# Layer 1 attention in a two-layer transformer kernel: where batch 0's queries are turned, and in which steps batch 1's queries and first maxima stand

## The reference, cut to what matters

```python
x = x + _L0_xattn_ref(_layernorm(x), ctx, ctx, mask0, ...)
x = x + _L0_ffn_ref(_layernorm(x), ...)          # 8 experts, one per token
x = x + _L1_xattn_ref(_layernorm(x), ctx, ctx, mask1, ...)
x = x + _L1_ffn_ref(_layernorm(x), ...)          # one shared, 7 routed experts, two per token

# layer 1 attention
q = layer_norm(query_antecedent @ Wq, gq, bq)    # per token, before the heads are split
k = layer_norm(key_antecedent @ Wk, gk, bk)
v = layer_norm(value_antecedent @ Wv, gv, bv)
sim = einsum('bhqd,bhkd->bhqk', qh / sqrt(dk), kh)
weights = softmax(sim + bias)                    # 16 heads of 16 channels
```

## Time and profile before

| | |
|---|---|
| median of three runs | 548.04 us |
| profiled execution | 548.11 us |
| its span, first to last instruction | 546.9 us |
| PE busy | 504.9 us, 92% |
| DVE busy | 261.6 us, 48% |
| ACT busy | 207.3 us, 38% |
| layer 0's FFN, last PE instruction | 219.58 us from the start |
| layer 1 attention, from its first top to the shared expert | 225.4 to 324.9 us |

### The profile page before, as it was taken

How to read it: one execution, slowest core, us unless ns; L and a number is a source line. 1 busy time by engine, 2 the same in 40 slices (tenths; PEclk the granted TensorE clock), 3 DMA queues, 4 the chain that set the end, 5 groups by cost and what they waited for, 6 DMA issues and landing times.

```text
span 546.9 us, 8791 instructions
## 1 busy us (share of the span) xinstructions
PE 504.9 (92%) x3285; PEld 373.3 (68%) x3285; DVE 261.6 (48%) x789; ACT 207.3 (38%) x425; POOL 82.2 (15%) x108
## 2 busy tenths in 40 slices
PE   2999999999889999679699998999999999999995
PEld 1456555645778999546356435656799999999994
DVE  5567798673337364365577826161322222222220
ACT  2434645462346653225466662220122222222221
POOL 2400700002102110200000000017212122212222
PEclk9999999997999999859899999999999999999999
DMA  8500005997113230380000012009786677666712
GB/s 299 188 1 0 2 1 164 369 373 224 59 38 104 72 97 20 99 296 1 0 2 2 1 39 77 1 10 362 269 282 201 202 238 248 211 200 220 251 13 33
DMA packets 42435, 72.06 MB, mean 132 GB/s; under 512 B 3405, under 2 KB 33037, under 8 KB 42384
## 3 DMA queue, kind: packets, MB, share of 16 engines
q1 hardware_dynamic: 33648, 60.65, 32.5%
q0 software_dynamic: 4336, 6.75, 5.6%
q10 hardware_dynamic: 4400, 4.01, 2.3%
HBM read 56.88 MB, written 14.51 MB: 131 GB/s over the span
## 4 chain that ended last, share of the span: by engine, by line
PE 57%; DVE 5%; DMA 3%; issue 2%; ACT 1%; POOL 1%; POOLq 0%; ACTq 0%; DVEq 0%
PE PS L1817 16%; PE PS L1832 9%; PE PS L1726 6%; PE PS L764 4%; PE PS L774 4%; PE PS L1737 3%; PE PS L1614 3%; PE PS L1603 3%; PE PS L795 2%; DVE W L956 2%; DMA VR<-scratch_rows 1%; PE PS L364 1%; PE PS L349 1%; PE PS L333 1%; PE PS L808 1%
## 5 line engine op out<-in xcount | busy, mean ns | idle before, releaser
L956 DVE TENSOR_REDUCE W<-PS 128x2 f32<-128x512 f32 x128 | 84.7, 687 | 41.3 <-PE PS L764 40.6
L1817 PE MATMUL PS<-PR,W 128*128 128x128 f32 x836 | 96.5, 275 | 0.0
L1817 PEld LDWEIGHTS PS<-PR,W 128*128 128x128 f32 x836 | 94.9, 192 | 0.1
L764 PE MATMUL PS<-W 32*128 32x256 f32 x512 | 85.7, 432 | 3.1 <-issue 1.6
L774 PE MATMUL PS<-W 32*128 32x512 f32 x256 | 84.3, 672 | 0.7 <-ACT W L1084 0.7
L764 PEld LDWEIGHTS PS<-W 32*128 32x128 f32 x512 | 56.4, 201 | 18.5 <-DVE W L956 9.0
L1832 PE MATMUL PS<-W,PR 128*128 x228 | 52.5, 380 | 0.8 <-ACT PR L2461 0.8
L2512 POOL DMA_INDIRECT out<-PR,slots x19 | 29.6, 1560 | 128.6 <-ACT PR L2461 125.4
L1084 ACT ACTIVATE PR<-PS 128x512 f32<-128x512 f32 x64 | 34.9, 595 | 30.8 <-PE PS L774 30.6
L1832 PEld LDWEIGHTS PS<-W,PR 128*128 128x128 f32 x228 | 41.9, 190 | 6.1 <-issue 1.2
L1084 ACT ACTIVATE W<-PS 128x512 f32<-128x512 f32 x64 | 34.7, 595 | 24.0 <-PE PS L774 24.0
(11 more groups left out here) (260 smaller groups left out, 625.5 us busy)
## 6 DMA issues: line engine op xcount, KB each, us to landing
W<-in_rguT SPq DMA_DIRECT2D x19, 1408.0 KB, 6.1
W<-in_L_ffn_W SPq DMA_DIRECT2D x16, 512.0 KB, 9.6
W<-in_rdT SPq DMA_DIRECT2D x5, 768.0 KB, 9.5
W<-in_mask SPq DMA_DIRECT2D x3, 1024.0 KB, 14.3
scratch_rows<-W SPq DMA_DIRECT2D x1, 2860.0 KB, 14.8
VR<-scratch_rows SPq DMA_DIRECT2D x19, 130.0 KB, 5.3
scratch_x<-W SPq DMA_DIRECT2D x1, 2048.0 KB, 14.1
PR<-scratch_x SPq DMA_DIRECT2D x16, 128.0 KB, 2.2
```

What stands on the lines that cost most here:

```text
L764: m = pe.matmul(PS[:, bank, q * FK:(q + 1) * FK], QT[r:r + 32, g, c:c + 128], KT[r:r + 32, g, b * FK:(b + 1) * FK], start=True, stop=True)
L956: dve.tensor_reduce(NM[:, s % 2, q:q + 2, c], PS[:, m_bank(use), :].rearrange("p (q n) -> p q n", q=2), AX, ALU.max).then_inc(sem("m_free" ...
L1817: m = pe.matmul(PS[:, bank, j * 128:(j + 1) * 128], W[:, o:o + 128], XS[:, r % 2, k, :], start=(k == 0), stop=(k == 1))
```

## The change

Four parts. **(a)** In layer 0's FFN the norms of batch 0's rows move from tile 12 to tile 11 and are shared by DVE and ACT, their turn to `beside(12)`, the projection to `mid(13)`, the second norms to `beside(13)`, and the four head groups are turned in tiles 14 and 15 instead of behind the fork. Three of four `mask_keys` go to tile 10, one to tile 14. **(b)** Batch 1's rows: the DVE pieces run on into step 0 (two per top), ACT's norms move to (0,1), the turn to (0,2), the projection to (1,0). **(c)** Batch 1's second norms and first head group move from (1,3) to (2,2), the second group stays in (2,3), third in (3,3), fourth in (4,3); the statistics of step 1 run two pieces per top from gap 1 on. **(d)** Step 4's first four tops move from gaps 2 and 3 of step 2 to step 3, whose gaps 0 and 1 then have four tops each. `pe_pairs` writes the gaps out; in gap 2 of every step of both layers a top now stands ahead of each weights job, as it did in gap 0.

```diff
-                (0, 7, 1): ["rows0_0_1"], (1, 0, 0): ["x1_1_1"]}
-    BESIDE_E = {..., (1, 0, 0): ["x1_1_0"], (1, 0, 2): ["q1_1_0", "q1_1_1"]}
-    BESIDE_E.update({(1, 1 + g, 3): [f"q1t1_{g}"] for g in range(NG)})
+                (0, 7, 1): ["rows0_0_1"], (1, 0, 2): ["x1_1_1"]}
+    BESIDE_E = {..., (1, 0, 2): ["x1_1_0"], (1, 1, 0): ["q1_1_0", "q1_1_1"],
+                (1, 2, 2): ["q1t1_0"], (1, 2, 3): ["q1t1_1"], (1, 3, 3): ["q1t1_2"], (1, 4, 3): ["q1t1_3"]}
+    def tops_of(l, n, gap):
+        if (l, n) == (1, 2) and gap > 1:
+            return []
+        if (l, n) == (1, 3) and gap < 2:
+            return [(4, i) for i in range(4 * gap, 4 * gap + 4)]
+        s, first = (n + 1, 4 + 2 * gap) if gap < 2 else (n + 2, 2 * gap - 4)
+        return [(s, i) for i in (first, first + 1) if s < STEPS]
...
+    def pe_pairs(l, n, gap):
+        tops = tops_of(l, n, gap)
+        if gap % 2:
+            pe_weights(l, n, 2 * gap)
+            pe_weights(l, n, 2 * gap + 1)
+            for s, i in tops:
+                pe_scores(l, s, i)
+            return
+        for k in range(2):
+            for s, i in tops[k:k + 1]:
+                pe_scores(l, s, i)
+            pe_weights(l, n, 2 * gap + k)
+        for s, i in tops[2:]:
+            pe_scores(l, s, i)
...
-    def dve_step(l, n, v, late):
+    def dve_step(l, n, v, late, pieces=1, since=0):
         for gap in range(4):
+            for s, i in tops_of(l, n, gap):
+                dve_top(l, s, i)
+                if gap >= since:
+                    for _ in range(pieces):
+                        next(late, None)
...
 act_beside, layer 1
-            if (n, gap) == (0, 0):
+            if (n, gap) == (0, 1):
+                act_x1(1)
+            elif (n, gap) == (0, 2):
                 act_xt_ring("x1_1", 1)
-            elif (n, gap) == (0, 2):
+            elif (n, gap) == (1, 0):
...
+            elif (n, gap) == (2, 2):
+                act.wait_ge(sem("stats"), NORMS[True]["q1_1"])
+                act.wait_ge(sem("wz"), 16)
+                for j in range(4):
+                    normal_act("q1_1", j, heads(RB[1][:, j, :]), by_head(RW[:, j, :])).then_inc(sem("q1_rows"), 1)
+                act_late_queries(0)
+            elif 2 <= n < 5 and gap == 3:
+                act_late_queries(n - 1)
...
 fast_pe, mid(i)
+            elif i == 13:
+                pe.wait_ge(sem("wp_2"), 16)
+                project_batch("q1_0", "x1_0", 2, 0)
+            elif i == 15:
+                claim(7, "q1t0_2")
+                filled(7, turned_heads(7, RB[0], 2))
+                pe.wait_ge(*at(1, "qt", 1))
+                turned_heads(5, RB[0], 3).then_inc(sem("q_ps"), 1)
 fast_pe, beside(i)
-            elif i == 13:
+            elif i == 12:
                 pe.wait_ge(sem("x1_rows"), 4)
                 turn_batch("x1_0", rows_for(0, 0))
             elif i == 14:
-                pe.wait_ge(sem("wp_2"), 16)
-                project_batch("q1_0", "x1_0", 2, 0)
+                taken(6, "q1_0")
+                taken(7, "q1_0")
+                turned_heads(5, RB[0], 0).then_inc(sem("q_ps"), 1)
+                claim(6, "q1t0_1")
+                filled(6, turned_heads(6, RB[0], 1))
...
+        pe.wait_ge(*at(1, "qt", 2))
+        taken(6, "q1t0_1")
+        taken(7, "q1t0_2")
         fork(pe, 0)
     def second_pe():
-        for g in range(NG):
-            turned_heads((5, 2, 0, 1)[g], RB[0], g).then_inc(sem("q_ps"), 1)
         pe_first(1)
...
 fast_act, beside(i)
+            elif i == 11:
+                act.wait_ge(sem("stats"), NORMS[True]["x1_0"])
+                for j in (2, 3):
+                    normal_act("x1_0", j, OB[:, 0, j, :], X[:, j, :]).then_inc(sem("x1_rows"), 1)
             elif i == 12:
-                act_x1(0)
+                act_xt("x1_0", (6,), 0)
             elif i == 13:
-                act_xt("x1_0", (6,), 0)
+                ...
+                normal_act("q1_0", 0, heads(RB[0][:, 0, :]), by_head(half(6, 0))).then_inc(sem("q1_half"), 1)
+                freed(6, normal_act("q1_0", 1, heads(RB[0][:, 1, :]), by_head(half(6, 1))))
+            elif i == 14:
+                queries_out(1, 0, 5).then_inc(sem("qt"), 1)
+                act.wait_ge(*full(6, "q1t0_1"))
+                freed(6, queries_turned(1, 0, 1, 6))
+            elif i == 15:
+                act.wait_ge(*full(7, "q1t0_2"))
+                freed(7, queries_turned(1, 0, 2, 7))
+                act.wait_ge(*at(1, "q_ps", 2))
+                queries_turned(1, 0, 3, 5).then_inc(sem("qt"), 1)
...
 second_act
-        for g in range(NG):
-            queries_out(1, g, (5, 2, 0, 1)[g]).then_inc(sem("qt"), 1)
         stored(act, TILES0)
-        act_x1(1)
 second_dve
-        dve_first(1, beside, late)
-        whole(late)
+        dve_first(1, nothing, begun)
         for s in range(8):
-            late = queries_norm() if s == 1 else rows_early() if s == 6 else empty
-            dve_step(1, s, v, late)
+            late = begun if s == 0 else queries_norm() if s == 1 else rows_early() if s == 6 else empty
+            dve_step(1, s, v, late, 2 if s < 2 else 1, 1 if s == 1 else 0)
```

More of the change, by code:

```diff
@@ L271, in ring_uses @@
             for n in range(STEPS):
-                tops = [("top", l, n + 1, i) for i in range(4, 8)] + [("top", l, n + 2, i) for i in range(4)]
                 for gap in range(4):
-                    m += [top for top in tops[2 * gap:2 * gap + 2] if top[2] < STEPS]
+                    m += [("top", l, s, i) for s, i in tops_of(l, n, gap)]
                     m += BESIDE_M.get((l, n, gap), [])
@@ L1035, in dve_beside @@
         else:
-            if (n, gap) == (0, 0):
+            if (n, gap) == (0, 2):
                 dve_xt_ring("x1_1", 1)
@@ L1039, in dve_beside @@
                 rows_taken_dve(1, 0)
-    def dve_step(l, n, v, late):
+    def dve_step(l, n, v, late, pieces=1, since=0):
         for gap in range(4):
[L1044 to L1048, removed]
+            for s, i in tops_of(l, n, gap):
[3 more added lines that the diff above has]
+                        next(late, None)
                 if gap == 1 and i == 6 and n > 1:
                     dve_divide(l, n - 2, v)
+            if gap == 1 and n > 1 and not tops_of(l, n, gap):
+                dve_divide(l, n - 2, v)
             if gap == 2 and n + 1 < STEPS:
@@ L1969, in again_pe @@
         pe.wait_ge(sem("again_rows"), 12)
+        for g in range(NG):
+            turned_heads((5, 2, 0, 1)[g], RB[0], g).then_inc(sem("again_turned"), 1)
+        pe.wait_ge(sem("again_xt"), 2 + NG)
     def second_pe():
-        for g in range(NG):
-            turned_heads((5, 2, 0, 1)[g], RB[0], g).then_inc(sem("q_ps"), 1)
         pe_first(1)
@@ L2058, in beside @@
                 settle(v, dve.tensor_scalar(masked1[:, :, :], masked1[:, :, :], 0.0, -1.0e30, ALU.is_equal, ALU.mult))
+            elif i == 10:
+                for n in range(3):
+                    dve.wait_ge(*at(1, "kt", n + 1))
+                    mask_keys(1, n)
             elif i == 11:
@@ L2062, in beside @@
                 whole(statistics(v, "x1_0", rows_of(0)))
+                for j in range(2):
+                    normal_dve("x1_0", j, OB[:, 0, j, :], X[:, j, :]).then_inc(sem("x1_rows"), 1)
             elif i == 12:
[L2064 to L2066 removed]
+                dve_xt("x1_0", 0)
             elif i == 13:
[L2068 to L2069 removed]
                 raw = [half(6 + j // 2, j) for j in range(4)]
                 whole(statistics(v, "q1_0", raw, True, [full(6 + j // 2, "q1_0") for j in range(4)]))
[L2073 to L2079 removed]
+                dve.wait_ge(sem("pads"), 3)
+                normal_dve("q1_0", 2, heads(RB[0][:, 2, :]), by_head(half(7, 2))).then_inc(*v.up())
+                freed(7, normal_dve("q1_0", 3, heads(RB[0][:, 3, :]), by_head(half(7, 3))))
+            elif i == 14:
+                dve.wait_ge(*at(1, "kt", 4))
+                mask_keys(1, 3)
+        ffn0_dve(MAIN, beside)
         fork(dve, 1, v)
@@ L2097, in second_dve @@
         empty = iter(())
-        late = queries_begun(v)
-        def beside(i):
-            if i > 2:
-                next(late, None)
         def queries_norm():
@@ L2179, in fast_act @@
         ffn0_act(MAIN, beside)
-        act.wait_ge(sem("stats"), NORMS[True]["q1_0"])
-        for j in range(2):
-            ins = normal_act("q1_0", j, heads(RB[0][:, j, :]), by_head(half(6, j)))
-            if j == 0:
-                ins.then_inc(sem("q1_half"), 1)
-        freed(6, ins)
         fork(act, 2)
@@ L2200, in again_act @@
             normal_act("q1_0", j, heads(RB[0][:, j, :]), by_head(half(6 + j // 2, j))).then_inc(sem("again_rows"), 1)
+        for g in range(NG):
+            act.wait_ge(sem("again_turned"), 3 + g)
+            queries_turned(1, 0, g, (5, 2, 0, 1)[g]).then_inc(sem("again_xt"), 1)
     def second_act():
-        for g in range(NG):
-            queries_out(1, g, (5, 2, 0, 1)[g]).then_inc(sem("qt"), 1)
         stored(act, TILES0)
```

(1 more changed line is left out.)

60 lines of the change are left out of this document (20 added, 40 removed).

## The result

The change made the kernel a little slower. Its median is 550.87 us (15 runs, 548.33 to 553.18) against 548.04 (15 runs, 546.09 to 552.12), and the ratio is 1.0042, 95% interval [1.0023, 1.0061]. The same kernel timed again beside later runs gave 1.0024 [0.9989, 1.006], which by itself can't be told from no change. The forecast was 5.4 us faster, so the prediction was wrong in its sign. The profiled execution took 550.92 us (span 549.7).

What follows compares the result with a forecast made beforehand. It took PE, waiting on chains of statistics, norms and turn, as the bound, with DVE setting the pace from 230 to 235 us. Wins of 2.6, then 4.7, then 5.4 us by step 4 gave 548.1 - 5.4 = 542.7 us, range 539.5 to 546.3.

Steps and rivals of the forecast that it cites:

- Waiting for the rows: Layer 0, after down(11): PE waits 0.3 us for the norms of batch 0's rows, ready at 202.2.
- some of the first eight ... will wait: Layer 1's first tops, no longer mixed with combines, make DVE wait: 0 to 2.5 us, taken as 1.5.
- the wait on the added maxima: Step 2's first weights wait for DVE's second statistics and added maximum: a new wait of 1.6 us, bounds 0 and 2.6.
- the wait was right: Step 2: PE waits 2.7 us for norms standing behind gap 2's exponentials, bounds 1.5 and 5.1.
- the rival of a second fall: New waits of 1.6 and 2.7 us make the clock fall around step 2: +2, 544.7 us; chance 0.17.
- the sign that the prediction named: A clock row below 0.9 after step 2's start would show the prediction wrong.
- Cost 2.3 us: Step 3's gaps 0 and 1, with eight reductions and a division, cost 2.3 us more; nearest bounds 0.8 and 4.
- The ring rule: Step 3: tops wait for banks, so the last goes out 5.3 us into the step; gaps 0 and 1 usually take 2.96.
- A clock that stays high: Rival: the clock stays high in layer 1's first phase, saving part b's 1.5 us: 541.2 us; chance 0.17.
- The long low stretch through steps 1 to 3 (558): Rival: PE stays at the low clock from the first phase through steps 1 to 3: +15, 558 us; chance 0.06.
- A slow DVE: Rival: 16 reductions in steps 1 and 3 cost 0.2 us more each, both maxima waits grow: +3.3, 546.0 us; chance 0.12.
- The reorder of gap 2: The new order in gap 2 of all 16 steps costs 0 us, bounds -1 and +1.

Runs made afterwards that it cites:

- mix_d: table_mix with part d added, the head group left in step 1's gap 3: ratio to the kernel before 0.9986 [0.9961, 1.0012].
- a_only: The changed kernel with parts b, c and d undone, the new order of gap 2 kept: ratio to the kernel before 0.9961 [0.9929, 0.9992].
- ab_table: ab with one added Exp on ACT, so the exponential's table loads before layer 1: ratio to the kernel before 0.9916 [0.9882, 0.9951].
- table_mix: ab_table with batch 1's combines begun behind step 0's sixth top, not the ninth reduction: ratio to the kernel before 0.9868 [0.9832, 0.9903], median 543.91 us.
- mix_all: table_mix with parts c and d added, so all four parts: ratio to the kernel before 0.9986 [0.9962, 1.001].
- ab_c21: ab with the second norms and first head group in step 2's gap 1, tops at old places: ratio to the kernel before 0.9951 [0.9923, 0.9978].
- mix_c21: table_mix with the second norms and first head group in step 2's gap 1: ratio to the kernel before 0.99 [0.9874, 0.9926].
- ab: The changed kernel with parts c and d undone: ratio to the kernel before 0.9946 [0.9921, 0.997].
- ab_d: The changed kernel without part c, the first head group turned in (1,3) again: ratio to the kernel before 1.0047 [1.0015, 1.0079].
- table_busy: ab_table with 40 added transposes of the identity on PE among the first tops and gaps of step 0: ratio to the kernel before 1.029 [1.025, 1.0329].
- after_rows: The changed kernel with step 3's tops ordered 0, 1, 4, 5 in gap 0 and 2, 3, 6, 7 in gap 1: ratio to the kernel before 0.999 [0.9966, 1.0014].

## Why the prediction was wrong

The forecast named moments; against those of the profiled execution the 8.2 us between 542.7 and 550.92 split as follows.

**Part a: right in mechanism and size.** Waiting for the rows cost 1.28 us instead of 0.3 (the fourth combine waited 1.14 us for a gathered row that the sum took as present), the fork 0.92 as taken. The twelve profiles that hold part a without that late row have 24.2 to 24.6 us from tile 12 to the first top against 27.1: 2.4 to 2.9 won, forecast 2.6. In this execution the first top came at 224.40, not 222.8; 1.6 us of the miss are here. 0.7 of it stood already when tile 11 began (195.13 instead of 194.47), the late row made the rest. It is late in mix_d too (1.21 us), and in no other profile. That slipping gathers cost nothing did not hold in a_only's profile, where the combines come early.

**Part b: a price left out, and one too small.** From the first top to the statistics' end the forecast has 19.4 us and the trace 22.3. The step that failed is "some of the first eight ... will wait: 0 to 2.5 us, I take 1.5". In the timeline DVE's idle times between its first reduction and the statistics' end sum to 3.9 us. The table load of 1.28 us was in no term. It had been hidden behind ACT's norms, and moving the norms uncovered it: 1.1 to 2.0 us (ab_table). Beginning the combines earlier brings the turn to the 21.7 us that the forecast had (table_mix), so the rest was DVE standing idle among tops that nothing was mixed with. By step 2's first weights the kernel is 2.5 us behind the forecast, the wait on the added maxima being 1.2 us, forecast 1.6.

**Part c: the wait was right, its tail was not.** PE waited 2.53 us, forecast 2.7. But step 2 then took 13.7 us (265.93 to 279.63) instead of 11.85. By the pieces of the timeline about 1.3 us of that is the low clock behind the wait (outputs 1.94 instead of 1.06, weights and head group slower in like measure), and about 0.6 is gap 0, whose first two weights run without the top that went ahead of them. So the rival of a second fall came in mechanism (+2 there, the whole 1.9 here with the other piece), and with it the sign that the prediction named, a clock below 0.9 after step 2's start. With it the part won nothing (mix_all against mix_d, and in its other form ab_c21 and mix_c21). That rival, with a chance of 0.17, belonged into the forecast: the clock had been at 0.50 behind the old 5.1 us wait too, and its own text said that step 2 has little work around the waits.

**Part d: the term that was mis-sized.** "Cost 2.3 us", bounds 0.8 and 4. This is the step that failed most clearly: the price is 4.4 us in this profile and 4.7 to 6.5 in the timed kernels. The ring rule was right, the last top waited 0.66 us for a bank. But the sum ended the price when that top goes out, 5.3 us into the step. It went out at 6.3 (285.95), since in gap 0 the third and fourth top already ran one behind the other and in gap 1 the first tops ran behind the weights; and its own time, 1.05 us until the outputs start at 287.00, was in no term. Those two pieces are the 2.1 us that are missing. The late top ran alone, 1.13 us for four matmuls where the three tops issued together took 1.15 for twelve. The lower bound of 0.8 us as four tops' own time was too low for the same reason. That the timed kernels say more than the profile fits a clock that falls within step 3 in part of the executions; how often it falls is not shown. No rival had that: each fall was tied to a wait of microseconds, and this one comes in a stretch with 4.95 of 5.50 us busy.

The four pieces 1.6, 2.5, 1.9 and 2.1 sum to 8.1 us. By the timed kernels, free of one profile's chances, the steps from the kernel before over ab and ab_d to the changed one are: a and b -0.54% (3.0 us), d +1.01% (5.5 us), c -0.05%. The forecast had 7.7 us won ahead of d's 2.3, so more than half of the miss, 4.5 us, lies in a to c, where 3.2 came.

**The rivals.** A clock that stays high: no, 0.50 from about 228 us to 252. The long low stretch through steps 1 to 3 (558) did not come either; the 2.9 us wait was followed by 0.60 in the mean of 248 to 253 us and 1.00 from 253 to 258; that rival's 3.5 us more for the projection was an estimate that no run shows, the projection took 3.72 us here (254.51) against 3.62 before. A slow DVE: not in this form. The wait for step 2's maxima was 1.2 us, under its forecast, and in step 3's gap 1 it is DVE that stands idle for 1.81 us until the three tops are there. (Its sum also counted 16 reductions where steps 1 and 3 have 6 and 8.) The reorder of gap 2 shows nothing: steps 4 to 7 last as before.

What stays open: why the clock falls in step 3's gap 1 in four profiles and not in the other three, and what c and d would cost with no wait of PE ahead of them at all. A version of d with a fourth bank in the M ring, which would take the wait away, was not tried, as all eight banks of the kernel's `PS` are in use.

## What to carry to other kernels

When work is moved away from in front of an instruction, list what was hidden behind it, one-time costs such as the table load of 1.28 us here among them, and give them a cheap early place. Ask of a job that is cheap beside its neighbours whether it is still issued with them: in gap 1 of step 3, with three banks for a burst of four tops, the first three took 1.15 us together and the fourth waited 0.66 us and took 1.13 alone. Bursts of three on rows that their neighbours leave free are what to try; the only burst of three run here was on shared rows in part, and it won nothing. And a term that is cheap "because it runs beside other work" deserves an upper bound at its price alone, also at the low clock: for a top 1.13 us at 1.00 and 2.07 at 0.50 here.

## What the runs showed of the hardware that was not expected

In these runs the granted clock did not follow from what the profile calls busy. In table_busy it stayed at 0.50 through 25 us with PE busy for 5.00 of every 5.00 us, mostly lone tops and transposes. In mix_d it fell from 1.00 to 0.50 in a stretch with 4.95 of 5.50 us busy. The changed kernel's first profile has the same order of work in step 3 and stays at 1.00 there, with PE busy for 3.34 of 4.00 us (283 to 287). So neither the busy share nor the order of work told which way it went, and no run here isolates the cause.

In the changed kernel's step 3 a top that ran alone took as long as three that ran together (1.13 and 1.15 us at 1.00), and tops issued on the rows of the weights ahead of them started 0.96 us after those, where in after_rows tops on other rows started 0.01 us after.
